# A two-layer message network and three graph attention layers on one core: messages by pairs of tiles, attention scores and row weights read from PSUM by VectorE

## The chip, the cores and the metric

The kernel runs on one core of one Trainium2 chip. The metric is the device time of one execution in microseconds (us). PE is TensorE, DVE is VectorE, ACT is ScalarE, POOL is GpSimd, and SP is the engine that issues most of the plain DMAs. A quad is four tiles of 128 edges, a pair is two tiles.

## The reference

The graph has 3125 nodes of 128 features and 100,000 edges. A residual network of two message layers comes first, and then a residual network of three GATv2 layers. The part of the reference that matters here:

```
def _block(h, src, dst, w, wm, bm, gm, bem, wu, bu, gu, beu, wg, bg):      # message layer, D = 160
    ecat = jnp.concatenate([h[src], h[dst]], axis=-1)
    em = jax.nn.relu(_layernorm(ecat @ wm.T + bm, gm, bem)) * w[:, None]
    msum = jax.ops.segment_sum(em, dst, num_segments=n)
    cnt = jax.ops.segment_sum(jnp.ones_like(w), dst, num_segments=n)[:, None]
    ...
def _gatv2_layer(x, src, dst, edge_e, Wl, bl, Wr, br, att_w, bias):        # 4 heads of 32
    gl = (x @ Wl + bl).reshape(n, HEADS, CH)
    gr = (x @ Wr + br).reshape(n, HEADS, CH)
    xj = gl[src]
    e = xj + gr[dst] + edge_e
    e = jax.nn.leaky_relu(e, negative_slope=0.2)
    alpha = jnp.einsum('ehc,hc->eh', e, att_w)
    m = jax.ops.segment_max(alpha, dst, num_segments=n)
    alpha = jnp.exp(alpha - m[dst])
    denom = jax.ops.segment_sum(alpha, dst, num_segments=n)
    alpha = alpha / (denom[dst] + 1e-16)
    out = jax.ops.segment_sum(xj * alpha[..., None], dst, num_segments=n)
    return out.reshape(n, HEADS * CH) + bias
```

## The kernel before

The program sorts the edges by destination once (0 to about 1600 us of the trace). After that each of the five edge layers walks the 812 tiles of 128 sorted edges in order, in 203 quads. The engines run programs written out by hand and meet only at semaphores, so that the order on each engine is the order of its source lines.

**Gathers.** For each tile POOL issues one indirect DMA that fetches 128 rows of a node table in HBM: L500 in the message layers (`ptab_d`, 160 columns), L508 in the attention layers (`gtab_d`, 132 columns). The gather of tile t waits until PE has summed quad t//4 - 8 (`s_sum` in the message layers, `s_e` in the attention layers), so that gathers run at most eight quads ahead.

**An attention layer** (`s_e` and the names below) runs in 217 rounds. In round j PE first does a step of a chunk's softmax if one is due. Then `scat` of quad j-14 (L1131) multiplies one-hot matrices by weighted rows into PSUM banks 6 and 7, after DVE has added what those banks held two pairs before (`s_acc2`). Then `pair(2j)` and `pair(2j+1)` follow: for each tile a matmul of a transposed one-hot with the node table block (L1144) and one that adds the gathered rows (L1147), 132 columns wide, into bank u % 3 for pair u. Each pair ends with a signal `s_e` and waits for the ACT copy of pair u-3 (`s_relu`). ACT copies the four linear columns (L876) and applies relu (L877) out of PSUM for each pair, converts the one-hots of quad j-12 (L892), and copies the row weights of quad j-13 from PSUM (L901). DVE multiplies gathered rows by weights (L1728, quad j-13), adds the four tiles of quad j-14 to the node sums (L1715), multiplies the relu by the attention vector (L1737) and reduces it to four scores for each edge (L1744). The softmax goes by chunks of eight quads: 26 chunks, whose steps (scans L1654 to L1657, carries L1667 to L1683, arguments L1690 to L1696, then the exponent and the weights' transpose) come in rounds 8c+9, +10, +11 and +12. Every second round begins on PE and on DVE with a load of eight register values (L426), the node block of each tile.

**A message layer** runs by quads: PE does `scat` of quad j-2 (L1061) and the sum of quad j (L1075 and L1078) into four banks. ACT takes the squares of each tile (L831) and one square root for the quad (L834), and scales the one-hots (L812). DVE does one reciprocal (L1539) and four normalising operations (L1545), then the adds (L1557).

**SP** loads the transposed one-hots and one-hots by eight tiles and, before the step of a chunk, that chunk's masks. The load of masks of chunk c waits until chunk c-2 is through.

Of the kernel before, what the change touches and what calls it, by code (L numbers as in the profile page):

```python
# [14 lines left out]
B = 112  # L15
# [8 lines left out]
NCH = (NQ + 7) // 8  # L24
TK = 32 * NCH
# [54 lines left out]
def gnn_program(nc, a, out):  # L80
    with ExitStack() as ctx:
# [12 lines left out]
        tabs_d = [nc.dram_tensor("ptab_d", (NP, D), F32).ap(), nc.dram_tensor("gtab_d", (NP, 132), F32).ap()]  # L94
# [7 lines left out]
        padc = sb("padc", [B, 1])  # L102
# [37 lines left out]
        BLb = carve(132, B)  # L140
        BRb = carve(132, B)
# [4 lines left out]
        attB = gB[:, 0:128]  # L146
        att2B = nbeB[:, 0:128]
        WLx = WPQ1[:, 0:132]
        WEx = WPQ1[0:16, D:D + 132]
# [5 lines left out]
        ring0 = cur[0]  # L155
        XJ = carve(32 * D)
        SQB = carve(6 * 512).rearrange("p (g k n) -> p g k n", g=6, k=4)
        NBB = carve(16 * B).bitcast(BF16).rearrange("p (g k n) -> p g k n", g=8, k=4)
        u0 = cur[0]
        RG = carve(4 * 8 * RW).rearrange("p (g t w) -> p g t w", g=4, w=RW)  # L160
        SW = carve(4 * 4 * B).rearrange("p (g k n) -> p g k n", g=4, k=4)
        VB = carve(3 * 644).rearrange("p (g k n) -> p g k n", g=3, k=4)
        JK = carve(D)
        SSQ = carve(4 * 8).rearrange("p (g n) -> p g n", g=4)
# [6 lines left out]
        RL = carve(2 * 512).rearrange("p (g n) -> p g n", g=2)  # L171
        AB = carve(2 * 528).rearrange("p (g k h c) -> p g k h c", g=2, k=4, h=4)
        PX = carve(3 * 528).rearrange("p (g k h c) -> p g k h c", g=3, k=4, h=4)
# [4 lines left out]
        PT = carve(2 * 128).rearrange("p (g n) -> p g n", g=2)  # L178
# [9 lines left out]
        SRC = carve(T).bitcast(I32)  # L188
        W = carve(T)
# [71 lines left out]
        HZ = AR[:, NB * 128:NB * 128 + 17 * 528]  # L261

        def xj2(t):

            s = (t // 4) % 24
            r = HZ[:, s * 528:(s + 1) * 528] if s < 17 else XJ[:, (s - 17) * 528:(s - 16) * 528]
            return r.rearrange("p (k f) -> p k f", k=4)
# [6 lines left out]
        TABG = tab_flat[:, 0:(NB + 1) * 132].rearrange("p (b f) -> p b f", f=132)  # L274
        Z132 = Z[:, :, 0:132]
# [5 lines left out]
        WRx = WU1[:, 0:132]  # L281
        gamB, betB, biB = guB[:, 0:128], beuB[:, 0:128], beB[:, 0:128]
        den = Zf[:, NB * 128:NB * 132].rearrange("p (b h) -> p b h", h=4)

# [12 lines left out]
        def bcF(v2):  # L297
# [26 lines left out]
        s_e, s_relu, s_att, s_lin = (sem(n) for n in ("s_e", "s_relu", "s_att", "s_lin"))  # L324
        s_at, s_s0, s_v, s_car, s_c, s_arg, s_pt, s_f, s_pb, s_r = (
            sem(n) for n in ("s_at", "s_s0", "s_v", "s_car", "s_c", "s_arg", "s_pt", "s_f", "s_pb", "s_r"))
        s_p, s_px, s_oh2, s_scat2, s_acc2, s_rs = (sem(n) for n in ("s_p", "s_px", "s_oh2", "s_scat2", "s_acc2", "s_rs"))
# [5 lines left out]
        def places(names):  # L333
# [13 lines left out]
        PL = places("ident0 ones ident iota dsti srci wraw padt0 padt1 padt lt0 lt rhs0 rhs iop pad0 pad tio onesN rmask0 rmask padc0 padc")  # L347
# [54 lines left out]
        def chunk_end(c):  # L402

            return min(8 * c + 8, NQ)
# [4 lines left out]
        def step_of(j, lag):  # L409

            c = (j - lag - 8) // 8
            return c if (j - lag) % 8 == 0 and 0 <= c < NCH else None

# [18 lines left out]
        def gpsimd_program(e):  # L432
# [3 lines left out]
            def mile(inst, name):  # L436
# [36 lines left out]
            mile(e.memset(padc[:, :], 0.0), "padc0")  # L473
            w.wait_own()
            mile(e.affine_select(out=padc[:, :], in_=padc[:, :], compare_op=ALU.is_gt, fill=BIG, base=LASTB,
                                 pattern=[[0, 1]], channel_multiplier=-1), "padc")
# [1372 lines left out]
```

## Time and profile before

| | before |
|---|---|
| runs | 8888.65, 8905.91, 8882.41 us |
| median | 8888.65 us |
| profiled execution | 8893.99 us |
| its span | 8891.9 us |
| busy in the span | PE 66%, weight loads 56%, DVE 51%, ACT 33%, POOL 53% |
| mean granted clock of TensorE | 0.831 |

The span runs from the first to the last instruction; the 2.1 us between it and the execution's own time lie around it. The profiled execution is 5.3 us above the median. Busy shares are means over a sort, two message layers, three attention layers and short stretches between them, so the profile is best read stage by stage.

### The profile page before, as it was taken

The page shows a single profiled execution, that of the slowest core. Times are in us where ns is not written, and L with a number is a line of the kernel's source. Part 1 is how long each engine was busy: PE and PEld are TensorE (multiplying, and loading weights), DVE is VectorE, ACT ScalarE, POOL GpSimd, SP SyncE. Part 2 cuts the span into 40 slices and gives each one's busy share as a digit, 9 for nine tenths or more (in the row PEclk, how much of TensorE's full clock was granted, in tenths as well). Part 3 has the DMA queues.
Part 4 walks back from the last instruction along what each step waited for, and adds up shares of the span by engine and source line. Part 5 has one row for each costly group of instructions (what it writes and reads, how often), then busy time and mean ns, then how long its engine had stood idle before and what let it go on. Part 6 is the DMA issues. An engine that isn't in the chain of part 4 may idle for free.

```text
span 8891.9 us, 116092 instructions
## 1 busy us (share of the span) xinstructions
PE 5832.2 (66%) x32977; PEld 4937.4 (56%) x32977; DVE 4515.0 (51%) x13873; ACT 2893.1 (33%) x12251; POOL 4707.3 (53%) x4869
## 2 busy tenths in 40 slices
PE   6544555677777867777775767763776673677775
PEld 5333333366767546666644666663666663666664
DVE  4222212255555446666643665664656664556666
ACT  2222221355555335555521222221222221222221
POOL 2665553366666046666505666634666652666660
PEclk9999999898888668888857888876888885788886
DMA  3000000333333134444403333332333341333331
GB/s 88 25 22 23 23 24 16 98 103 103 102 104 101 18 93 118 122 119 117 104 4 95 116 103 115 115 72 71 107 110 116 102 108 50 103 115 115 103 116 28
DMA packets 389512, 753.22 MB, mean 85 GB/s; under 512 B 101824, under 2 KB 248433, under 8 KB 388121
## 3 DMA queue, kind: packets, MB, share of 16 engines
q0 software_dynamic: 180928, 305.59, 14.7%
q1 hardware_dynamic: 203610, 425.90, 13.9%
q10 hardware_dynamic: 4352, 14.30, 0.6%
q8 instruction: 284, 4.65, 0.2%
q14 instruction: 338, 2.77, 0.1%
HBM read 639.02 MB, written 105.63 MB: 84 GB/s over the span
## 4 chain that ended last, share of the span: by engine, by line
PE 32%; another core or an unknown queue 23%; DVE 18%; issue 12%; ACT 12%; DVEq 2%; DMA 1%; ACTq 0%; SPq 0%; POOL 0%; POOLq 0%
PE PS L1131 5%; PE PS L1147 4%; ACT AR L831 4%; PE PS L1144 4%; PE PS L950 3%; DVE AR L1715 3%; PE PS L1061 2%; DVE AR L1737 2%; PE PS L1078 2%; PE PS L1075 2%; DVE AR L1557 2%; ACT AR L812 2%; DVE AR L1545 2%; DVE AR L1728 2%
## 5 line engine op out<-in xcount | busy, mean ns | idle before, releaser
L508 POOL DMA_INDIRECT AR<-gtab_d,AR x2436 | 2364.1, 970 | 1925.9 <-issue 642.2
L500 POOL DMA_INDIRECT AR<-ptab_d,AR x1624 | 1558.1, 959 | 1394.2 <-issue 415.1
L1131 PE MATMUL PS<-AR 128*112 128x132 f32 x4872 | 964.8, 342 | 604.9 <-DVE AR L1715 366.1
L1144 PE MATMUL PS<-AR 128*128 x4872 | 1182.3, 331 | 268.9 <-issue 141.6
L1131 PEld LDWEIGHTS PS<-AR 128*112 128x112 f32 x4872 | 766.7, 218 | 751.7 <-issue 512.5
L1147 PE MATMUL PS<-AR,ident 128*128 128x132 f32 x4872 | 1137.5, 321 | 23.2 <-DMA AR<-gtab_d,AR 13.5
L485 POOL DMA_INDIRECT rec_d<-AR x782 | 775.0, 991 | 662.3 <-DVE AR L1322 234.8
L1144 PEld LDWEIGHTS PS<-AR 128*128 128x128 f32 x4872 | 945.5, 239 | 315.0 <-issue 313.2
L1061 PE MATMUL PS<-AR 128*112 128x161 f32 x3248 | 697.7, 355 | 624.5 <-DVE AR L1557 334.6
L876 ACT ACTIVATE AR<-PS 128x8 f32<-128x8 f32 x1218 | 227.2, 187 | 2652.7 <-remote 1341.8
L1715 DVE TENSOR_TENSOR AR<-AR,PS 112x132 f32 x2436 | 710.2, 292 | 747.8 <-remote 247.4
L1147 PEld LDWEIGHTS PS<-AR,ident 128*128 128x128 f32 x4872 | 934.1, 236 | 28.8 <-DMA AR<-gtab_d,AR 16.3
L1061 PEld LDWEIGHTS PS<-AR 128*112 128x112 f32 x3248 | 534.2, 204 | 745.3 <-issue 357.5
L1075 PE MATMUL PS<-AR 112*128 x3248 | 825.9, 339 | 40.7 <-issue 22.3
L1737 DVE TENSOR_TENSOR AR<-AR 128x512 f32<-128x512 f32 x609 | 420.5, 690 | 814.7 <-ACT AR L877 503.9
L1078 PE MATMUL PS<-AR,ident 128*128 128x160 f32 x3248 | 797.2, 330 | 19.5 <-issue 19.4
L831 ACT ACTIVATE AR<-PS 128x160 f32<-128x160 f32 x1624 | 494.4, 304 | 961.8 <-remote 581.1
L1557 DVE TENSOR_TENSOR AR<-AR,PS 112x161 f32 x1624 | 522.8, 322 | 525.4 <-remote 261.0
L950 PE MATMUL PS<-AR 128*56 128x168 bf16 (+3 forms) x1369 | 379.3, 432 | 447.0 <-DVE AR L1338 322.3
L1075 PEld LDWEIGHTS PS<-AR 112*128 112x128 f32 x3248 | 631.7, 223 | 61.8 <-issue 61.7
L1078 PEld LDWEIGHTS PS<-AR,ident 128*128 128x128 f32 x3248 | 619.5, 219 | 22.3 <-issue 22.1
L950 PEld LDWEIGHTS PS<-AR 128*56 128x56 bf16 x1369 | 219.3, 191 | 564.1 <-DVE AR L1338 328.3
(323 smaller groups left out, 8832.2 us busy)
## 6 DMA issues: line engine op xcount, KB each, us to landing
AR<-ste_d SPq DMA_DIRECT2D x404, 512.0 KB
AR<-nbb_d SPq DMA_DIRECT2D x303, 224.0 KB
ste_d<-AR SPq DMA_DIRECT2D x101, 512.0 KB
AR<-gtab_d,AR POOLq DMA_INDIRECT x2436
AR<-ptab_d,AR POOLq DMA_INDIRECT x1624
nbb_d<-AR SPq DMA_DIRECT2D x101, 224.0 KB
AR<-key_d SPq DMA_DIRECT2D x94, 224.0 KB
rec_d<-AR POOLq DMA_INDIRECT x782
```

Source lines behind the costliest of these rows:

```text
L485: e.indirect_dma_start(out=rec_d[:, :], out_offset=bass.IndirectOffsetOnAxis(ap=rowi[:, n:n + 1], axis=0), in_=REC[:, c * RW:(c + 1) * RW] ...
L500: e.indirect_dma_start(out=XJ1[:, t % 32, :], out_offset=None, in_=tabs_d[0][:, :], in_offset=off).then_inc(done_, 16)
L508: e.indirect_dma_start(out=xj2(t)[:, t % 4, :], out_offset=None, in_=tabs_d[1][:, :], in_offset=off).then_inc(done_, 16)
L831: done(e.activation(JK, PS[(t // 2) % 4][:, (t % 2) * D:(t % 2 + 1) * D], ACT.Square, accum_out=SSQ[:, j % 4, kk:kk + 1]))
L950: return e.matmul(PS[3][0:KD, r0 * KD:r1 * KD].rearrange("p (k n) -> p k n", n=KD), x[:, 0:KD], x[:, KD:112].unsqueeze(1).to_broadcast([12 ...
L1061: x = e.matmul(PS[4 + v_ % 2][0:B, (t % 2) * 161:(t % 2 + 1) * 161], SW[:, i % 4, t % 4, :], VB[:, i % 3, t % 4, :], start=True, stop=True ...
L1075: e.matmul(o, STE[0:B, ste_slot(l, t), (t % 8) * 128:(t % 8 + 1) * 128], TABQ[0:B, bass.ds(block_of(cp, "tensor", t), 1), :], start=True, ...
L1078: x = e.matmul(o, ident[:, :], XJ1[:, t % 32, :], start=False, stop=True, skip_group_check=True)
L1131: x = e.matmul(PS[6 + v_ % 2][0:B, (t % 2) * 132:(t % 2 + 1) * 132], SQB[:, i % 6, t % 4, 0:B], PX[:, i % 3, t % 4, :, :].rearrange("p h c ...
L1144: e.matmul(o, STE[:, ste_slot(l + 2, t), (t % 8) * 128:(t % 8 + 1) * 128], TABG[:, bass.ds(block_of(cp, "tensor", t), 1), :], start=True, ...
L1147: x = e.matmul(o, ident[:, :], xj2(t)[:, t % 4, :], start=False, stop=True, skip_group_check=True)
L1715: x = e.tensor_tensor(o, o, PS[6 + v_ % 2][0:B, (t % 2) * 132:(t % 2 + 1) * 132].rearrange("p (a h c) -> p a h c", a=1, h=4), ALU.add)
```

## The change

**Attention layers.** The tables grow from 132 to 140 columns (`GW`): 35 for each head, which are 32 values, a column that holds one, and the linear sum with both signs. With an attention vector whose last three entries are 0, 1 and -1, a score is the sum of max(x, 0) times that vector, so that one DVE instruction for each pair (L1761 of the changed kernel, 128x280, input in PSUM) takes the place of L876, L877 and L1737. The product with the row weights (L1751) reads the weights in PSUM and writes 33 columns for each head, and L901 goes. PE's pairs wait for that DVE instruction, four banks deep (`s_att` of pair u-4), instead of for ACT's relu, three deep. The reduce (L1769) now reads 560 columns, and stands ahead of the adds. PX has five slots instead of three, and 29 quads of gathered rows are kept instead of 24. There are 27 chunks; the steps of a chunk lie two rounds apart, one round apart in the last four chunks, and the last chunks have four, four and three quads. Quad i is weighted in round i+17 (two in a round from round 193 on), where it was i+13; the layer has 214 rounds instead of 217. Mask loads stand elsewhere in SP's order.

**Message layers.** `scat`, the sums, the squares, the square root, the reciprocal and the adds go by pairs: `scat` of pair u-4 and the sum of pair u on PE, a square root and a reciprocal for each pair, adds of pair u-3. Making the masks is spread over the layer by sevens instead of eights.

```diff
-                for j in range(NQ + 14):
-                    for lag, step in ((1, scans), (2, carries), (3, args)):
+                for j in range(LASTR):
+                    for n, step in ((0, scans), (1, carries), (2, args)):
...
-                        w.wait_ge(s_p, quad_at(l, i))
+                        t0 = 4 * (i - chunk_start(chunk_of(i)))
+                        w.wait_ge(s_r, chunk_at(l, chunk_of(i)))
+                        if i >= 5:
+                            w.wait_ge(s_scat2, pair_at(l, 2 * (i - 5) + 1))
                         done(e.tensor_tensor(
-                            PX[:, i % 3, :, :, 0:32], xj2(4 * i)[:, :, 0:128].rearrange("p k (h c) -> p k h c", h=4),
-                            PX[:, i % 3, :, :, 32:33].to_broadcast([128, 4, 4, 32]), ALU.mult), s_px)
-                    if 14 <= j:
-                        add_quad(j - 14)
+                            PX[:, i % 5, :, :, :], xj2(4 * i).rearrange("p k (h c) -> p k h c", h=4)[:, :, :, 0:33],
+                            PS[4][:, 0:128].rearrange("p (h t) -> p t h", h=4)[:, t0:t0 + 4, :].unsqueeze(3).to_broadcast([128, 4, 4, 33]),
+                            ALU.mult), s_px)
                     if j < NQ:
-                        w.wait_ge(s_relu, pair_at(l, 2 * j + 1))
...
-                        done(e.tensor_tensor(
-                            AB[:, j % 2, :, :, 0:32], RL[:, j % 2, :].rearrange("p (k h c) -> p k h c", k=4, h=4),
-                            attB.unsqueeze(1).to_broadcast([128, 4, 128]).rearrange("p k (h c) -> p k h c", h=4), ALU.mult), s_att)
...
+                        for u in (2 * j, 2 * j + 1):
+                            w.wait_ge(s_e, pair_at(l, u))
...
+                            done(e.scalar_tensor_tensor(
+                                AB[:, j % 2, kk:kk + 2, :], PS[u % 4][:, 0:2 * GW].rearrange("p (k f) -> p k f", k=2), 0.0,
+                                attB.unsqueeze(1).to_broadcast([128, 2, GW]), ALU.max, ALU.mult), s_att)
...
+                    for i in weighted_in(j - 1):
+                        add_quad(i)
```

```diff
                     def pair(u):
-                        if u >= 3:
-                            w.wait_ge(s_relu, pair_at(l, u - 3))
+                        if u >= 4:
+                            w.wait_ge(s_att, pair_at(l, u - 4))
...
+def rounds_of_attention():
+    ends = list(range(8, 193, 8)) + [196, 200, NQ]
+    px, steps, start = [], [], 0
+    for c, end in enumerate(ends):
+        gap = 2 if c < 23 else 1
+        turn = end + gap
+        if steps:
+            turn = max(turn, steps[-1][2] + 1)
+        back = max(turn + 2 * gap + 1 + gap, px[-1] + 1 if px else 0)
+        steps.append((turn, turn + gap, turn + 2 * gap, turn + 2 * gap + gap - 1, back))
...
                         if t >= 32:
-                            w.wait_ge(s_sum, quad_at(layer, t // 4 - 8))
+                            w.wait_ge(s_sum, pair_at(layer, 2 * (t // 4 - 8) + 1))
```

On DVE, the middle of the first attention layer, before: a round's scores, product and adds, then the register load of the next round and its first add.

```order
L1737 TENSOR_TENSOR AR<-AR 128x16x32
L1744 TENSOR_REDUCE AR<-AR 128x4x4
L1728 TENSOR_TENSOR AR<-AR 128x16x32
L1715 ISA
L1715 TENSOR_TENSOR AR<-AR,PS6 112x132
```

The same place in the changed kernel (L1751 is the product, L1761 the score instruction of a pair, L1769 the reduce, L1735 an add):

```order
L1751 TENSOR_TENSOR AR<-AR,PS4 128x528
L1761 SCALAR_TENSOR_TENSOR AR<-PS0,AR 128x280
L1761 SCALAR_TENSOR_TENSOR AR<-PS1,AR 128x280
L1769 TENSOR_REDUCE AR<-AR 128x4x4
L466 TENSOR_LOAD AR
L1735 ISA
L1735 TENSOR_TENSOR AR<-AR,PS6 112x132
```

The scores read PSUM directly, a pair at a time, and the adds moved behind them.

On PE in the same stretch, before: `scat` of both pairs, the register load, and the first tile of the next quad.

```order
L1131 MATMUL PS6<-AR 112x132 x2
L1131 MATMUL PS7<-AR 112x132 x2
L426 TENSOR_LOAD AR
L1144 ISA
L1144 MATMUL PS0<-AR 128x132
L1147 MATMUL PS0<-AR,ident 128x132
```

In the changed kernel:

```order
L1145 MATMUL PS6<-AR 112x132 x2
L1145 MATMUL PS7<-AR 112x132 x2
L466 TENSOR_LOAD AR
L1158 ISA
L1158 MATMUL PS0<-AR 128x140
L1161 MATMUL PS0<-AR,ident 128x140
```

The order is the same; the pairs are 140 columns wide and go round four banks.

## Rows read from the trace of the kernel before

**Rows 1.** Busy time by stretch: a message layer, the second, an attention layer, its end.

```profile
core 0: us, PE busy (x) PEld busy (x) DVE busy (x) ACT busy (x) POOL busy (x), PEclk, DMA share, GB/s
1667.00:2940.00 1273.00, 945.81 (x5632) 865.75 (x5632) 683.95 (x2617) 735.84 (x3025) 769.01 (x801) 0.88 0.34 100
3197.00:4436.00 1239.00, 892.87 (x4882) 823.43 (x4882) 744.80 (x2979) 703.92 (x2850) 758.92 (x794) 0.85 0.41 116
4703.00:5993.00 1290.00, 879.82 (x5222) 790.82 (x5221) 742.82 (x1890) 293.14 (x1270) 784.39 (x805) 0.80 0.35 103
...
5911.00:5993.00 82.00, 58.91 (x318) 50.20 (x317) 57.30 (x163) 20.66 (x76) 0.00 (x0) 0.73 0.19 44
```

**Rows 2.** POOL's groups, 4800 to 5900 us (attention) and 1700 to 2900 us (messages).

```profile
L508 POOL DMA_INDIRECT AR<-gtab_d,AR x730 | 712.7, 976 | 386.1 <-issue 192.3 <-remote 108.5 <-PE PS L1147 82.9
...
L500 POOL DMA_INDIRECT AR<-ptab_d,AR x773 | 742.7, 961 | 460.4 <-issue 191.9 <-remote 175.8 <-PE PS L1078 92.7
```

**Rows 3.** POOL's timeline: start, duration, idle before it; three runs begin, one ends.

```profile
5012.81 0.94 POOL L508 DMA_INDIRECT AR<-gtab_d,AR  x1 [1.76 <-remote]
...
5021.68 0.95 POOL L508 DMA_INDIRECT AR<-gtab_d,AR  x1 [0.30 <-issue]
5024.65 0.95 POOL L508 DMA_INDIRECT AR<-gtab_d,AR  x1 [2.02 <-remote]
...
5036.49 0.95 POOL L508 DMA_INDIRECT AR<-gtab_d,AR  x1 [1.55 <-remote]
```

**Rows 4.** PE's timeline, the last pair of a quad.

```profile
5032.53 0.39 PE L1147 MATMUL PS<-AR,ident 128*128 128x132 f32 x2
```

**Rows 5.** ACT's timeline, the first instruction after that quad's pairs, both pairs.

```profile
5036.17 0.18 ACT L876 ACTIVATE AR<-PS 128x8 f32<-128x8 f32 x1 [8.04 <-remote]
...
5036.50 0.19 ACT L876 ACTIVATE AR<-PS 128x8 f32<-128x8 f32 x1
```

**Rows 6.** ACT's timeline at the start of the first attention layer.

```profile
4719.26 0.18 ACT L876 ACTIVATE AR<-PS 128x8 f32<-128x8 f32 x1 [11.53 <-remote]
...
4739.59 0.19 ACT L876 ACTIVATE AR<-PS 128x8 f32<-128x8 f32 x1 [19.88 <-remote]
...
4750.80 0.18 ACT L876 ACTIVATE AR<-PS 128x8 f32<-128x8 f32 x1 [10.75 <-remote]
```

**Rows 7.** POOL's timeline: the end and the beginning of its first pause there.

```profile
4743.32 0.95 POOL L508 DMA_INDIRECT AR<-gtab_d,AR  x1 [0.31 <-issue]
4751.03 0.94 POOL L508 DMA_INDIRECT AR<-gtab_d,AR  x1 [6.77 <-remote]
```

**Rows 8.** Waits, 4800 to 5900 us: us in total, times, longest.

```profile
ACT AR L876 <- remote: 378.5, 64, 8.5
ACT AR L876 <- PE PS L1147: 328.5, 142, 8.4
```

**Rows 9.** DVE's groups, 4800 to 5900 us.

```profile
L1715 DVE TENSOR_TENSOR AR<-AR,PS 112x132 f32 x720 | 209.9, 292 | 228.5 <-remote 90.9 <-issue 66.3 <-DVE AR L1715 41.7
L1744 DVE TENSOR_REDUCE AR<-AR 128x16 f32<-128x528 f32 x182 | 128.4, 705 | 6.2
L1737 DVE TENSOR_TENSOR AR<-AR 128x512 f32<-128x512 f32 x182 | 125.7, 690 | 175.4 <-ACT AR L877 90.8 <-issue 83.2
L1728 DVE TENSOR_TENSOR AR<-AR 128x512 f32<-128x512 f32 x181 | 123.6, 683 | 22.4 <-issue 22.4
...
L1657 DVE TENSOR_TENSOR AR<-AR 128x128 f32<-128x128 f32 x23 | 6.8, 294 | 0.8
L1696 DVE TENSOR_TENSOR AR<-PS,AR 128x128 f32<-128x128 f32 x23 | 6.7, 293 | 0.8
```

**Rows 10.** Groups of the message layer, 1700 to 2900 us: DVE's reciprocal, ACT's square root.

```profile
L1539 DVE RECIPROCAL AR<-AR 128x4 f32<-128x4 f32 x193 | 33.9, 176 | 247.3 <-ACT AR L834 230.1 <-issue 17.2
...
L834 ACT ACTIVATE AR<-AR,eps 128x4 f32<-128x4 f32 x193 | 57.7, 299 | 6.3
```

**Rows 11.** What SP's queue waited for, 4800 to 5900 us.

```profile
SPq L64 <- PE PS L1179: 375.0, 10, 39.3
```

More of the change, by code:

```diff
@@ L23 @@
 NG = (NQ + 1) // 2
-NCH = (NQ + 7) // 8
-TK = 32 * NCH
+HW = 35
+GW = 4 * HW
+TK = T + 32
+NXJ = 29
+def rounds_of_attention():
[8 more added lines that the diff above has]
+        steps.append((turn, turn + gap, turn + 2 * gap, turn + 2 * gap + gap - 1, back))
+        for i in range(start, end):
+            r = max(back + 1 - (c < 23), px[-1] if px else 0)
+            while px.count(r) >= (1 if r < NQ - 10 else 2):
+                r += 1
+            px.append(r)
+        start = end
+    return ends, steps, px
+ENDS, STEPS, PXR = rounds_of_attention()
+NCH = len(ENDS)
+LASTR = PXR[-1] + 3
 ROWS = 128 * T
@@ L139, in gnn_program @@
         WPQ2 = carve(2 * D, 33)
-        BLb = carve(132, B)
-        BRb = carve(132, B)
+        BLb = carve(GW, B)
+        BRb = carve(GW, B)
         BPQ = BLb[0:1, :]
@@ L400, in half, with chunk_start, chunk_of, step_of @@
             return min(8, T - 8 * g8)
-        def chunk_end(c):
-            return min(8 * c + 8, NQ)
+        def chunk_start(c):
+            return ENDS[c - 1] if c else 0
+        def chunk_of(i):
+            return next(c for c in range(NCH) if i < ENDS[c])
         def chunk_at(layer, c):
             return layer * NCH + c + 1 if c >= 0 else 0
-        def step_of(j, lag):
-            c = (j - lag - 8) // 8
-            return c if (j - lag) % 8 == 0 and 0 <= c < NCH else None
+        def step_of(j, n):
+            return next((c for c in range(NCH) if STEPS[c][n] == j), None)
+        def weighted_in(j):
+            return [i for i in range(NQ) if PXR[i] == j]
         def load_of(c):
@@ L603, in sync_program @@
                     e.dma_start(LD[:, 0:T], DL[127:128, :]).then_inc(s_lk, 16)
-                    for g8 in range(NG + 8):
+                    for g8 in range(NG + 10):
                         if g8 < NG:
@@ L649, in sync_program @@
                         read_ste(e, w, l + 2, g8)
-                    if g8 == 0 or g8 % 4 == 2 and g8 // 4 + 1 < NCH:
-                        load_masks(e, w, l, 0 if g8 == 0 else g8 // 4 + 1)
-                    o8 = g8 - 5
+                    if g8 < 2:
+                        load_masks(e, w, l, g8)
+                    for c in range(2, NCH):
+                        if g8 == (4 * c + 4 if c < 24 else 100 + 2 * (c - 24)):
+                            load_masks(e, w, l, c)
+                    o8 = g8 - 7
                     if o8 >= 0:
@@ L1499, in tile_rows @@
                     w.wait_own()
-                    for x, r in ((AM, 0), (E2, 31), (EM, 31)):
-                        v(e.memset(x.rearrange("p (c t) -> p c t", t=32)[:, :, r:r + 1], BIG))
+                    for end in ENDS:
+                        v(e.memset(AM[:, 4 * end:4 * end + 1], BIG))
+                        for x in (E2, EM):
+                            v(e.memset(x[:, 4 * end - 1:4 * end], BIG))
+                    v(e.memset(AM[:, 0:1], BIG))
+                    for x in (E2, EM):
+                        v(e.memset(x[:, TK - 1:TK], BIG))
                     w.wait_own()
@@ L1558, in vector_program @@
                                 acc_done = w.done(x, s_acc if t % 2 else None)
+                        if 0 <= u < 2 * NQ:
+                            w.wait_ge(s_rms, pair_at(l, u))
+                            v(e.reciprocal(SSQ[:, u % 8, 0:2], SSQ[:, u % 8, 2:4]))
+                            if u >= 6:
+                                w.wait_ge(s_scat, pair_at(l, u - 6))
+                            w.wait_own()
+                            for t in (2 * u, 2 * u + 1):
+                                x = e.scalar_tensor_tensor(
+                                    VB[:, u % 6, t % 2, 0:D], PS[u % 4][:, (t % 2) * D:(t % 2 + 1) * D],
+                                    SSQ[:, u % 8, t % 2:t % 2 + 1], nbeB, ALU.mult, ALU.max)
+                            done(x, s_vt)
                 w.wait_ge(s_tab, 16 * (l + 1))
```

351 lines of the change are left out of this document (159 added, 192 removed), and 6 rows, old and new, of the table DV.

## The prediction

> **What bounds the kernel now.** I read the busy times by stretch first, to see whether any engine is full. None is: in an attention layer of 1290 us PE is busy for 880, DVE for 743, POOL for 784 and ACT for 293, and in a message layer of 1273 us no engine reaches 950 [rows 1]. So the pace is set by engines waiting for one another, and the next view is POOL's, since POOL does the same work in all five edge layers. 730 gathers in 1100 us are 12.05 us for eight (two quads, 6.03 us each); the 773 of the message layer in 1200 us are 12.42 us for eight, 6.21 each [rows 2]. The two kinds of layer have quite different work on PE, ACT and DVE, and yet nearly the same pace. Of each period the gathers themselves take 8 x 1.25 = 10.0 us, and then POOL stands still for about 2 us until PE has signalled the quad that frees the next slots: runs begin at 5012.81, 5024.65 and 5036.49 us, twice exactly 11.84 us apart [rows 3].
>
> Why is PE's signal late? PE's last pair of a quad stands in the trace at 5032.53 us and ends at 5032.92 [rows 4]. ACT, which has nothing else to do, starts on the first pair of that quad at 5036.17 and on the second at 5036.50, after 8.04 us of idleness [rows 5]. At least 0.9 us of matmuls lie between the two pairs on PE; their signals reach ACT 0.33 us apart or closer. So it is not the matmuls that are late but what others see of them, and it comes out in a bunch just before POOL starts again. The start of a layer shows the same without the pauses: POOL issues gathers without a stop until 4744.3 us [rows 7], and ACT gets to a pair after 11.5, 19.9 and 10.8 us of waiting, at 4719.26, 4739.59 and 4750.80 [rows 6]; then all is ready at once and POOL goes on at 4751.03. In the largest waits of the layer ACT waits 378.5 us for a releaser that the trace doesn't name, and 328.5 us for L1147 [rows 8]; that is 707 of 1100 us.
>
> My reading, which the trace suggests but doesn't prove: while POOL issues gathers back to back, PE's progress is seen late, and POOL must pause for PE to catch up. Eight gathers and one pause make 12 us, whatever DVE and ACT do in between. The change leaves the gathers, the eight-quad window and PE's order as they are.
>
> **The change part by part, attention layers.** Two rows price DVE's new shapes: 512 columns take 0.690 us (L1737), 128 columns 0.294 us (L1657), so 1.03 ns a column [rows 9]. A score instruction of 280 columns is then 0.294 + 152 x 0.00103 = 0.451 us; it reads PSUM, which costs nothing more, since L1696 (PSUM) takes 0.293 us where L1657 (SBUF) takes 0.294 for the same 128 columns [rows 9]. The reduce grows by 32 columns (+0.033) and the product by 16 (+0.017). For each quad DVE loses L1737 (0.690) and gains 0.902 + 0.050: +0.262 us, 53 us for 203 quads. DVE's occupancy now is 743/203 = 3.66 us of work and, in the stretch of rows 9, 108 us of short gaps at L1715 over 182 quads, 0.59: 4.25 of 6.03 us. It becomes 4.5, still below the 5.0 of four gathers. I count these 53 us at nothing, because the idle 1.8 us a quad covers them; if the cover is gone they cost 53 us a layer.
>
> The Trainium skill, "VectorE: DVE Perf Modes", section on the TRN2 errata, gives a PSUM source 62 cycles more of fixed cost on VectorE than an SBUF source. By that page the two score instructions and nothing else would be some 0.13 us a quad dearer, 26 us a layer; L1696 against L1657 contradicts it here.
>
> ACT loses L876, L877 and L901. It was waiting 707 us anyway [rows 8], so the direct worth is nothing; what could be worth something is the hop, PE to ACT to DVE, which becomes PE to DVE. That shortens what follows the late signal by one relu pair and adds nothing to when the signal comes. PE gets four banks instead of three for pairs. Its pairs are 140 instead of 132 columns: two thirds of its matmuls get 6% longer, 880 x 2/3 x 0.06 = 35 us a layer of busy time, beside 410 us idle. The mask loads leave SP blocked for 375 us of 1100 [rows 11]; no engine's largest wait is for what SP loads, so moving them is worth nothing. Chunk steps two rounds apart spread DVE's work: 743 - 203 x (4 x 0.292 + 0.705 + 0.690 + 0.683) = 84 us, 3.2 us for each of 26 chunks. They are off the path while gathers run.
>
> **The end of a layer** has no gathers, and there DVE counts. The window from the landing of the last gather to the last add is 82 us; DVE is busy for 57.3 [rows 1], and with 22 quads of adds at 0.59 us of gaps it is occupied for 70. At that point before has 22 quads to weight and add (the lag is 14 rounds); the change has 25 (17 rounds and one). That is 3 x (0.70 + 4 x 0.292 + 0.59) = 7.4 us, one more chunk's steps 3.2, and 8 rounds of scores at 0.26, 2.1: +12.7 us of DVE's work, of which the 12 idle us may hide some. I take 11 a layer, bounds 0 and 15 (with 6% of PE's 59 us), 33 in all. Packing two quads to a round from round 193 shortens the count of rounds by three, not the work.
>
> **Between the layers** the weights' preparation has some 14 more small DVE instructions in series. The nearest row is the reciprocal of 4 columns, 0.176 us [rows 10]: 2.5 us a layer, 7.5 in all; bounds 0 and, with the weight loads in 32-column pieces, 6 a layer.
>
> **Message layers.** A second reciprocal (0.176) on DVE and a second square root (0.299) on ACT for each quad [rows 10] are 36 and 61 us a layer, beside 589 and 537 us idle [rows 1]: nothing. Working by pairs ends the layer perhaps half a quad earlier, 3 us; bounds 0 and 6. The gathers wait for the same quad as before.
>
> **Sum.** 8894.0 + 33 + 7.5 - 6 = 8928.5 against the profiled execution; that one lies 5.3 us above the median of the runs, so 8923.
>
> **Rivals.** *The chain was the bound (faster).* If the period is in truth the round trip PE, ACT, DVE, PE, the change cuts a hop out of it, adds a bank, and by pairs does the same for the messages. For it: ACT waits for L1147 in 328.5 us, and no engine is full. Against it: the equal period of unlike layers, 11.84 us twice to the hundredth, and the bunched signals. Rounds of 5.5 us, halfway between 6.0 and the gathers' 5.0, give 3 x 195 x 0.53 = 310 us and in the messages 195 x (0.71 + 0.6) = 255 (the second message layer at 6.1 by its 1239 us): 8923 - 565 = 8358. With the gathers as the only bound it would be 7870; with a pause a tenth of a microsecond or two shorter, some 8800.
>
> *The late signals starve DVE (slower).* DVE now meets PE directly: it can't score before `s_e` is seen, PE's banks stay taken until it has, and it stands in order before the adds that free `scat`'s banks. If of each 12 us DVE can work only the 8 or so between a late bunch and the next, its 9.0 us for two quads no longer fit in the round that also carries a chunk's step, and its added 53 us come out in full: 3 x 53 = 159, 9082; with PE's 35 a layer as well, 9187. It decides when the slack of 1.5 us a quad is less than what DVE must wait for PE.
>
> *The change does less than it says.* DVE's reduce, product and adds stay in one queue, so that dropping ACT's work moves no wait. That is the forecast.
>
> **How the numbers follow.** Pace kept, 0.45: 8880 to 8960, of which two fifths lie within 0.3% of before (26.7 us, about what a measurement of this kernel can tell from no change) and nearly all the rest above. Chain, 0.35: 7870 to 8860. Starved DVE, 0.20: 8960 to 9190. Together: faster 0.36, same 0.20, slower 0.44. The likeliest is 8923. The range has to leave out no more than 2 in 10: below 8400 I see 0.13 and above 9120 0.05, so 8400 to 9120.
>
> **What would show it.** If the pace is kept, eight gathers take 11.8 to 12.1 us in the changed kernel's attention layers, POOL's pause stays near 2 us, DVE rather than ACT shows the long waits for PE (over 250 us in 1100), and the end of a layer grows from 82 to about 93 us. The chain rival shows in runs of more than eight gathers, or pauses under 1 us. The starved DVE shows in pauses of 3 us with DVE busy before them. I am wrong if the 280-column instruction takes over 0.6 us, or if PE's banks, not its signals, were what POOL waited for.

## The result, and the profile after

The changed kernel takes 9004.36 us (median of four runs, 8999.17 to 9005.93) beside 8895.42 us for the kernel before (8882.41 to 8905.91): ratio 1.0122, 95% interval 1.0105 to 1.014. It is slower by 1.2%. The forecast was 8923 us, slower, in a range of 8400 to 9120. The direction is right and the time lies in the range, but the loss is three times the one that was summed up: 105 us between the profiled executions, where the sum had 34.5.

| us, profiled executions | before | after | difference |
|---|---|---|---|
| gathers, first to last, message layer 1 | 1251.1 | 1300.2 | +49.1 |
| the same, message layer 2 | 1227.6 | 1236.4 | +8.8 |
| the same, three attention layers | 3645.9 | 3588.7 | -57.2 |
| last gather to last add, three attention layers | 240.6 | 336.0 | +95.4 |
| last add to the next layer's first gather, twice, or to the end | 307.8 | 314.7 | +6.9 |
| last gather to last add, two message layers | 78.6 | 72.3 | -6.3 |
| everything else (the sort, +4.6; the stretch ahead of the first attention layer, +4.2) | | | +8.6 |
| span | 8891.9 | 8997.2 | +105.3 |

Three rows carry it, and they have different signs: the first message layer's gathers and the ends of the attention layers are longer, and the attention layers' gathers are shorter. The busy times of the changed kernel by stretch, in the columns of [rows 1]: the two message layers, the first attention layer, and that layer's end.

```profile
1672.00:2992.00 1320.00, 914.33 (x5638) 875.01 (x5638) 718.28 (x2823) 796.73 (x3230) 759.30 (x801) 0.85 0.34 96
3238.00:4494.00 1256.00, 862.16 (x4897) 796.11 (x4896) 779.01 (x3290) 764.80 (x3057) 759.82 (x801) 0.86 0.40 115
4755.00:6064.00 1309.00, 897.80 (x5250) 794.86 (x5250) 779.04 (x2111) 122.15 (x258) 765.95 (x812) 0.82 0.36 105
5953.00:6064.00 111.00, 70.38 (x383) 60.38 (x381) 71.66 (x213) 14.73 (x32) 0.00 (x0) 0.75 0.12 23
```

No engine is full here either. ACT has fallen from 293 to 122 us in the attention layer, and the layer is 19 us longer.

POOL's group in the changed kernel, 4860 to 5940 us, answers to [rows 2]:

```profile
L544 POOL DMA_INDIRECT AR<-gtab_d,AR x730 | 688.7, 943 | 392.0 <-issue 195.4 <-remote 126.1 <-PE PS L1161 70.6
```

It is 730 gathers in 1080 us, 11.84 us for eight; the pauses for PE (126.1 + 70.6 us) are as long as before (108.5 + 82.9; over all three layers POOL's idle time beyond the usual 0.3 us between gathers is 551 us where it was 543), but the mean gather is 943 ns, where it was 976. POOL's timeline, against [rows 3]:

```profile
5001.66 0.94 POOL L544 DMA_INDIRECT AR<-gtab_d,AR  x1 [0.30 <-issue]
5004.83 0.94 POOL L544 DMA_INDIRECT AR<-gtab_d,AR  x1 [2.23 <-remote]
...
5013.56 0.94 POOL L544 DMA_INDIRECT AR<-gtab_d,AR  x1 [0.30 <-issue]
5016.68 0.94 POOL L544 DMA_INDIRECT AR<-gtab_d,AR  x1 [2.17 <-remote]
```

Eight gathers, a pause of 2.2 us, a period of 11.85 us: the pace is kept. Who waits has changed. In the waits of 4860 to 5940 us DVE now meets PE's late signal itself, 226 us in all, where ACT waited 707 us [rows 8]:

```profile
DVE AR L1761 <- PE PS L1161: 124.8, 46, 5.9
...
DVE AR L1761 <- remote: 101.3, 47, 5.9
```

DVE's new shapes, by its groups in the same stretch, against [rows 9]:

```profile
L1761 DVE SCALAR_TENSOR_TENSOR AR<-PS,AR 128x280 f32<-128x280 f32 x362 | 145.4, 442 | 226.3 <-PE PS L1161 124.8 <-remote 101.3 <-issue 0.3
L1769 DVE TENSOR_REDUCE AR<-AR 128x16 f32<-128x560 f32 x181 | 133.7, 739 | 6.2
L1751 DVE TENSOR_TENSOR AR<-AR,PS 128x528 f32<-128x528 f32 x176 | 122.4, 696 | 0.1
```

They came out at 0.442, 0.739 and 0.696 us, and were priced at 0.451, 0.738 and 0.700.

### The profile page after: what moved, and what is told of

It is laid out like the page before. It is cut to its first block, busy times and chain, and to the rows that moved or that the text cites. A ratio compares the mean times of both kernels' runs of the same rounds, so it can differ in the third digit from the quotient of the medians.

```text
span 8997.2 us, 115195 instructions
## 1 busy us (share of the span) xinstructions
PE 5829.8 (65%) x33021; PEld 4939.4 (55%) x33021; DVE 4690.3 (52%) x15073; ACT 2500.8 (28%) x9619; POOL 4620.2 (51%) x4867
## 4 chain that ended last, share of the span: by engine, by line
PE 18%; DVE 17%; issue 14%; another core or an unknown queue 10%; ACT 3%; DVEq 2%; DMA 1%; SPq 0%; ACTq 0%
PE PS L1145 4%; DVE AR L1735 4%; PE PS L1161 4%; PE PS L1158 3%; DVE AR L1761 2%; DVE AR L1751 2%; PE PS L1075 1%; DVE AR L1562 1%; DVEq L466 1%; PE PS L1092 1%; DVEq L1735 1%; PE PS L1089 1%; ACT AR L872 1%; DVE AR L1494 1%
## 5 line engine op out<-in xcount | busy, mean ns | idle before, releaser
L544 POOL DMA_INDIRECT AR<-gtab_d,AR x2436 | 2298.4, 944 | 2005.2 <-DMA gtab_d<-AR 712.1
L1158 PE MATMUL PS<-AR 128*128 x4872 | 1202.6, 334 | 255.1 <-issue 174.1
L1161 PE MATMUL PS<-AR,ident 128*128 128x140 f32 x4872 | 1167.9, 324 | 86.9 <-issue 68.6
L1735 DVE TENSOR_TENSOR AR<-AR,PS 112x132 f32 x2436 | 709.9, 291 | 603.1 <-DVE AR L1735 247.1
L1761 DVE SCALAR_TENSOR_TENSOR AR<-PS,AR 128x280 f32<-128x280 f32 x1218 | 491.4, 442 | 968.6 <-remote 499.4
L919 ACT ACTIVATE AR<-AR 128x448 f32<-128x448 bf16 x609 | 336.4, 571 | 1944.7 <-remote 1171.9
L1089 PE MATMUL PS<-AR 112*128 x3248 | 803.8, 332 | 32.5 <-issue 32.0
L1089 PEld LDWEIGHTS PS<-AR 112*128 112x128 f32 x3248 | 613.4, 217 | 47.5 <-issue 45.4
L1571 DVE SCALAR_TENSOR_TENSOR AR<-PS,AR 128x160 f32<-128x160 f32 x1624 | 549.2, 380 | 33.6 <-remote 3.2
```

Source lines behind the costliest of these rows:

```text
L544: e.indirect_dma_start(out=xj2(t)[:, t % 4, :], out_offset=None, in_=tabs_d[1][:, :], in_offset=off).then_inc(done_, 16)
L1089: e.matmul(o, STE[0:B, ste_slot(l, t), (t % 8) * 128:(t % 8 + 1) * 128], TABQ[0:B, bass.ds(block_of(cp, "tensor", t), 1), :], start=True, ...
L1158: e.matmul(o, STE[:, ste_slot(l + 2, t), (t % 8) * 128:(t % 8 + 1) * 128], TABG[:, bass.ds(block_of(cp, "tensor", t), 1), :], start=True, ...
L1161: x = e.matmul(o, ident[:, :], xj2(t)[:, t % 4, :], start=False, stop=True, skip_group_check=True)
L1735: x = e.tensor_tensor(o, o, PS[6 + v_ % 2][0:B, (t % 2) * 132:(t % 2 + 1) * 132].rearrange("p (a h c) -> p a h c", a=1, h=4), ALU.add)
L1761: done(e.scalar_tensor_tensor(AB[:, j % 2, kk:kk + 2, :], PS[u % 4][:, 0:2 * GW].rearrange("p (k f) -> p k f", k=2), 0.0, attB.unsqueeze(1 ...
```

## The experiments

The runs fell on at least three chips, which are of two kinds, and this has to be known first. On that of the measurement above and of the first four experiments (called chip A, a single chip or ones that run alike) the kernel before takes 8882 to 8936 us. On the two other chips (B for the next four, C for the last four) it takes 7387 to 7418 us. Only ratios to the kernel before on the same chip are compared across them.

**Plain loads instead of gathers** (chip A). ACT issues the loads of the attention layers; what they fetch is not what the edges need.

```diff
+                        r = 37 * t % 2880
+                        e.dma_start(xj2(t)[:, t % 4, :], tabs_d[1][r:r + 128, :]).then_inc(s_pl[(l * NQ + i) % 8], 16)
...
-                        e.indirect_dma_start(out=xj2(t)[:, t % 4, :], out_offset=None, in_=tabs_d[1][:, :],
-                                             in_offset=off).then_inc(done_, 16)
```

> The changed kernel, in whose attention layers ACT issues plain DMAs of 128 neighbouring rows of the table (same bytes, slots and window of eight quads) in place of POOL's indirect gathers; the rows are not those of the edges. The message layers keep POOL's gathers. Theory A (POOL's issuing of gathers is what makes PE's signals late): without it the 203 quads of an attention layer go at 4.5 to 5.0 us each instead of 5.93, so that the stretch from the first to the last load falls from 1196 to 900 to 1000 us a layer, and DVE's long waits for PE go. Theory B (the round trip between PE and DVE sets the pace, whoever loads): 1170 to 1210 us a layer, unchanged.

Measured: 8088.43 us, 916 less than the changed kernel. DVE's reduces, one for each quad, come every 4.66 to 4.69 us between quads 20 and 190 instead of every 5.93. In DVE's groups of 4900 to 5500 us (129 quads) the wait of the score instruction for PE has shrunk to 5.5 us:

```profile
L1775 DVE SCALAR_TENSOR_TENSOR AR<-PS,AR 128x280 f32<-128x280 f32 x258 | 103.8, 439 | 5.6 <-PE PS L1175 5.5
L1783 DVE TENSOR_REDUCE AR<-AR 128x16 f32<-128x560 f32 x129 | 95.3, 738 | 4.4
```

The signals themselves can be timed in the trace, from the end of a pair's last matmul to the start of the instruction that waits for it. Here 99 of the 100 waits of the score instruction end 0.04 us behind the matmul; in the changed kernel 243 of 331 end more than 3.5 us behind. So on this chip PE's signals are late with POOL's gathers and in time without them, the bytes, slots and window being the same. DVE is then the bound: of the 600 us it is busy or in the short gaps before its adds for all but some 16, at 4.66 us a quad, which the prediction had at 4.5. The run changes three things at once, though: the engine that issues, the kind of DMA (indirect or plain), and the rows (scattered or neighbouring). Which of them makes the signals late isn't separated; theory A names the first.

**A window of ten quads** (chip A).

```diff
-                        if t >= 32:
-                            w.wait_ge(s_e, pair_at(layer - 2, 2 * (t // 4 - 8) + 1))
+                        if t >= 40:
+                            w.wait_ge(s_e, pair_at(layer - 2, 2 * (t // 4 - 10) + 1))
```

> The changed kernel with gathers of the attention layers allowed ten quads ahead of PE instead of eight (40 semaphores instead of 32). Theory A: after a longer first run (48 gathers without a pause instead of 40) the same 11.8 to 11.9 us for eight gathers, since POOL still has to stop for PE; 1190 to 1200 us a layer. Theory B, or a latency from a gather's issue to its use that the window must cover: 1/5 shorter, down to the 10.0 us of the gathers alone; 1010 to 1100 us a layer.

Measured: 9051.61 us. POOL's group, 4870 to 5950 us:

```profile
L544 POOL DMA_INDIRECT AR<-gtab_d,AR x727 | 687.7, 946 | 392.9 <-issue 194.5 <-remote 136.7 <-PE PS L1161 61.7
```

The pace is the same (11.88 us for eight; 1198 to 1200 us a layer), and from the last gather to the last add it is 122 us instead of 112. A latency that the window has to cover is ruled out: it forecast 1010 to 1100 us a layer. More slots only leave more quads to finish when the gathers are over.

**A fixed node block on PE** (chip A), so that PE loads no register values in the attention layers; the scores are those of wrong nodes.

```diff
-                                     TABG[:, bass.ds(block_of(cp, "tensor", t), 1), :], start=True, stop=False, skip_group_check=True)
+                                     TABG[:, 0:1, :], start=True, stop=False, skip_group_check=True)
```

> The changed kernel, in whose attention layers PE takes block 0 of the node table for every tile, so that its loads of eight register values (every second quad) and its register operations go; scores are those of other nodes. Theory C (PE's loads of register values are what gets stuck while POOL issues, since the late pairs are those behind such a load): the late signals go and eight gathers take 10.0 to 10.8 us, 1010 to 1090 us a layer. Theory A in general: unchanged, 1185 to 1197 us.

Measured: 9009.15 us, 1195 to 1197 us a layer, and in POOL's group (4860 to 5940 us) the same pauses. PE's register loads are not what makes the signals late.

```profile
L544 POOL DMA_INDIRECT AR<-gtab_d,AR x730 | 690.7, 946 | 390.2 <-issue 193.9 <-remote 131.7 <-PE PS L1161 63.4
```

**Message layers by quads again** (chip A, timed). The parts of PE, ACT and DVE in the message layers, and the gather's wait, are put back as before:

```diff
-                            w.wait_ge(s_sum, pair_at(layer, 2 * (t // 4 - 8) + 1))
+                            w.wait_ge(s_sum, quad_at(layer, t // 4 - 8))
...
-                        done(e.activation(SSQ[:, u % 8, 2:4], SSQ[:, u % 8, 0:2], ACT.Sqrt, bias=eps[:, :], scale=1.0 / D), s_rms)
+                        done(e.activation(SSQ[:, j % 4, 4:8], SSQ[:, j % 4, 0:4], ACT.Sqrt, bias=eps[:, :], scale=1.0 / D), s_rms)
```

> The changed kernel with the message layers' sums, squares, roots, reciprocals and adds by quads, as before; the attention layers as changed. If working by pairs is what made the first message layer longer (gathers 1251 us before, 1300 us after; the second 1228 and 1236), they go back to 1245 to 1255 and 1225 to 1231 us and the kernel takes 8940 to 8955 us, ratio to before 1.005 to 1.007. If the masks by sevens or the memory's new layout did it: no change, ratio 1.011 to 1.013.

Measured: 8968.47 us, ratio 1.0067 (1.0045 to 1.009); the layers' gathers take 1250.8 and 1232.9 us. The ratio and the first layer are as expected; the second layer (1225 to 1231 us expected) and the time (8940 to 8955) came out a little longer. Nearly half of the loss belongs to the pairs, and nearly all of that to the first message layer. POOL's group in that layer, 1700 to 2900 us, of the changed kernel and of this run:

```profile
L536 POOL DMA_INDIRECT AR<-ptab_d,AR x741 | 703.3, 949 | 497.2 <-PE PS L1092 198.8 <-issue 181.7 <-remote 116.7
```

```profile
L536 POOL DMA_INDIRECT AR<-ptab_d,AR x774 | 736.7, 952 | 464.2 <-issue 192.3 <-remote 182.7 <-PE PS L1089 89.2
```

The pauses are 315 us for 741 gathers by pairs and 272 for 774 by quads.

**A window of six quads** (chip B, timed).

```diff
-                        if t >= 32:
-                            w.wait_ge(s_e, pair_at(layer - 2, 2 * (t // 4 - 8) + 1))
+                        if t >= 24:
+                            w.wait_ge(s_e, pair_at(layer - 2, 2 * (t // 4 - 6) + 1))
```

> The changed kernel with gathers of the attention layers allowed six quads ahead of PE instead of eight. Theory A (POOL pauses because PE's signals come late while it issues, not for lack of slots): the period of eight gathers stays 11.8 to 11.95 us, and a layer ends sooner, because only six quads instead of eight are left to score after the last gather: 2 x 4.9 = 10 us a layer, as ten quads cost 12 more. From the last gather to the last add 100 us instead of 112; kernel 8965 to 8980 us, ratio to before 1.006 to 1.008. Theory B (the window must cover a latency): the period grows by up to a third, 12.5 us or more, and the kernel takes over 9050 us.

Measured: 7371.58 us, ratio 0.9961 (0.9947 to 0.9975). POOL doesn't pause at all on this chip: eight gathers in 9.99 us, 1014 us a layer. The window is never reached, so this run can't answer its question, and nothing of the 10 us a layer that were expected of it can come: the changed kernel on chip C has 80.5 us from last gather to last add and this one 81.

**Chunk steps one round apart** (chip B, timed).

```diff
-        gap = 2 if c < 23 else 1
+        gap = 1
```

> The changed kernel with the steps of a chunk one round apart in all chunks, so that quad i is weighted in round i+13 as before; 27 chunks with the small last ones stay. If the lag of 17 rounds is what makes a layer's end longer (four quads more to weight and add, 4 x 2.45 us): the stretch from the last gather to the last add falls from 112 to 100 to 103 us, and gathers keep 11.8 to 11.95 us for eight; kernel 8970 to 8985 us, ratio 1.006 to 1.009. If the two rounds were needed to keep DVE clear of PE: eight gathers take 12.1 us or more and the kernel 9020 us.

Measured: 7341.19 us, ratio 0.9918 (0.9902 to 0.9935). From the last gather to the last add it is 69.3 us, 11 less than the changed kernel's 80.5 on chip C (and the 81 of the run before on this chip), and the gathers keep 1014 us. The lag of four more rounds costs 11 us a layer and buys nothing where this could be seen. On chip A it wasn't run.

**One more DVE instruction, with one input in SBUF, and with two** (chip B).

```diff
+                        if 1 <= j < 190:
+                            x = AB[:, j % 2, :, :]
+                            v(e.tensor_reduce(JUNK[:, 0:16], x.rearrange("p k (h c) -> p (k h) c", h=4), AX.X, ALU.add))
```

> The changed kernel with one more DVE instruction in each round of an attention layer up to round 189, a reduce of 560 columns with one input in SBUF, 0.74 us, whose result is not used (and a wait for DVE's own work). Theory A: DVE's 4.7 us of work a quad become 5.4, still under the 5.93 of the gathers' pace: gathers 11.85 to 12.2 us for eight. If DVE is the bound beside POOL: 0.7 us more a quad, 13.3 us for eight. Gathers keep their mean of 0.944 us.

```diff
+                            v(e.tensor_tensor(JUNK.bitcast(BF16), x.rearrange("p k f -> p (k f)")[:, 0:512], x.rearrange("p k f -> p (k f)")[:, 48:560], ALU.add))
```

> The same with a DVE addition of 512 columns whose two inputs are in SBUF, 0.69 us, like L1737 of the kernel before. If such an instruction holds up POOL's gathers (before: 98 gathers of over 1.1 us in the attention layers, the changed kernel none): 80 to 150 gathers of over 1.1 us come back in the attention layers and their mean rises from 0.944 to 0.965 to 0.985 us. If they came from something else: none, as in the run with one input.

Measured: 7509.91 and 7491.08 us. With one input the reduces of quads 20 to 190 come every 5.26 to 5.28 us instead of 4.99 to 5.00, and POOL pauses 17 to 19 times a layer, 14 to 15 us in all. The added instruction's 0.73 us a quad came out as 0.27, so on this chip DVE had less than 0.5 us a quad to spare before it is the bound. (The 11.85 and 13.3 us for eight gathers that were expected belong to chip A.) With two inputs the gathers themselves grow. The attention gathers of the whole trace, one input and then two:

```profile
L545 POOL DMA_INDIRECT AR<-gtab_d,AR x2436 | 2304.0, 946 | 1480.1 <-issue 695.3 <-DMA gtab_d<-AR 694.3 <-PE PS L1162 77.5
```

```profile
L545 POOL DMA_INDIRECT AR<-gtab_d,AR x2436 | 2336.5, 959 | 1430.3 <-issue 702.9 <-DMA gtab_d<-AR 688.2 <-PE PS L1162 26.1
```

6 gathers of over 1.1 us with one input, 95 with two. The mean rose by 13 ns, less than the 21 expected at least, the count fell within what was expected. So DVE instructions with two SBUF inputs hold up gathers. The timeline shows which ones: all 88 gathers that began 0.1 to 0.4 us after the start of the added two-input instruction took over 1.1 us, and none of the 95 that began so behind the added one-input instruction. The Trainium skill, "SBUF — State Buffer", section "SBUF: two separate sides", has the rule: VectorE and GpSimd share a pair of ports by an exclusive lock, which a VectorE instruction with two SBUF inputs takes against a GpSimd instruction that reads SBUF. By that rule, the trace agrees as far as the gathers go: in the trace of before 94 of the 98 long attention gathers ran beside L1737, whose two inputs lie in SBUF, and the other 4 beside L1728, which has two as well; the changed kernel's L1761 and L1751 take one input from PSUM, and none of its 2436 attention gathers there is over 1.1 us. DVE's side shows no hold-up: the 609 L1737 of before took 0.68 to 0.73 us each, those that began while a gather was under way too.

**The changed kernel, and the kernel before** (chip C, the first timed).

> The changed kernel itself, beside the kernel before on one chip, because chips differ: on one, before takes 8890 to 8910 us and POOL pauses 2 us after every eight gathers; on another it takes 7396 us and POOL does not pause. Where POOL pauses: ratio 1.010 to 1.014. Where it does not, the attention layers' gathers take 1014 us in both kernels, DVE's chain can't be the bound in either, and only the ends of the layers differ (some 15 to 30 us each) and the message layers' do not: ratio 1.005 to 1.013. If dropping ACT from the chain had a worth that the pauses hid, the ratio there is under 1.000.

> The kernel before itself, for its trace on the same chip as the others. Where POOL does not pause: eight gathers in 10.0 to 10.1 us in all five layers, save for gathers held up beside two-input instructions of DVE (mean 0.97 us instead of 0.945, 20 us a layer); from the last gather to the last add 60 to 75 us. Where it pauses: 11.9 us and 80 to 82 us.

Measured: 7363.26 us for the changed kernel beside 7395.6, ratio 0.9951 (0.9933 to 0.9969): on this chip it is the faster one, where 1.005 to 1.013 was expected. The trace of before (7393.15 us) shows ACT's and POOL's waits of 3900 to 4800 us so:

```profile
ACT AR L876 <- PE PS L1147: 562.8, 316, 5.3
POOL AR L508 <- issue: 202.7, 665, 0.3
PEld PS L1147 <- DMA AR<-gtab_d,AR: 154.0, 166, 2.9
```

POOL waits for nobody, and PE waits for gathers. In this trace each of the 1107 relu instructions that followed idleness came 0.04 us behind PE's last matmul; on chip A, of 793 such a quarter came more than 3.5 us behind, and the latest 39 us. The late signals aren't there on chips B and C, although POOL issues its gathers there with even fewer pauses; in the changed kernel too every wait for a pair ends 0.04 us behind it. The gathers of the two kernels, 3900 to 4800 and 3900 to 4750 us:

```profile
L508 POOL DMA_INDIRECT AR<-gtab_d,AR x702 | 685.9, 977 | 214.0 <-issue 202.7 <-PE PS L1147 9.1 <-DVE AR L1728 2.1
```

```profile
L544 POOL DMA_INDIRECT AR<-gtab_d,AR x681 | 643.4, 945 | 207.6 <-issue 195.7 <-PE PS L1161 10.1 <-DVE AR L1751 1.8
```

On this chip 181 of before's attention gathers are over 1.1 us, 3 of the changed kernel's. 32 ns a gather are 26 us a layer: 1040.6 us from first to last gather before, 1013.6 after, -81 for three. The message layers' gathers go from 1031.7 to 1017.6 us, -28 for two. The layers' ends take that back in part: 55.8 us before, 80.5 after, +74 for three. With 5.5 us between the layers the sum is -29.5; -32.3 was measured. My expectation there had left out the gathers held up by DVE, though I had written them into the next one; that one had them at 0.97 us and 20 us a layer, and had 60 to 75 us for the layers' ends, which are 55.8. Its other outcome, a ratio under 1.000 because ACT is out of the chain, gets no support: POOL waits for nobody in either kernel here, and the shorter gathers make up the gain.

**The message layers by quads and the steps one round apart, with 27 chunks and then with 26** (chip C, timed).

```diff
+                    if 1 <= j <= NQ:
+                        i = j - 1
+                        w.wait_ge(s_rms, quad_at(l, i))
...
-        gap = 2 if c < 23 else 1
+        gap = 1
```

> The changed kernel with the message layers by quads as before and the chunk steps one round apart; 27 chunks. Both undone parts cost something in the runs so far (0.55% for the pairs where POOL pauses; the steps' lag at the ends of the layers). Sum of the two where POOL pauses: 8967 - 3 x 10 = 8937 us, ratio 1.002 to 1.006, 112 us from the last gather to the last add down to 100. Where it does not pause: ratio 0.988 to 0.995, since before's gathers are held up there by DVE and the new kernel's are not.

```diff
-    ends = list(range(8, 193, 8)) + [196, 200, NQ]
+    ends = list(range(8, 201, 8)) + [NQ]
```

> The same with 26 chunks, the last of 8, 8 and 3 quads as before, instead of 27 with 4, 4 and 3 at the end. If the four chunk steps packed into the last rounds are what makes the end long (3.2 us of DVE and a round of waits for PE for each): another 5 to 15 us off each layer's end, and the kernel 15 to 40 us faster than the run with 27 chunks; 1.000 to 1.003 of before where POOL pauses. If the small last chunks are worth having, because weights come earlier: 5 to 10 us a layer slower than it.

Measured: 7366.01 us (ratio 0.9955, 0.9941 to 0.9969) and 7354.70 us (0.9932, 0.9909 to 0.9956). Both end the layers sooner, 69.2 and 65.0 us against 80.5. Both expectations were a little too good: the first ratio was to be 0.988 to 0.995, and 26 chunks were to take another 5 to 15 us off each end and 15 to 40 off the time, where 4 and 11 were measured. The last gather and the last adds of the first attention layer with 26 chunks:

```profile
4821.36 0.94 POOL L544 DMA_INDIRECT AR<-gtab_d,AR  x1 [0.30 <-issue]
```

```profile
4887.12 0.29 DVE L1734 TENSOR_TENSOR AR<-AR,PS 112x132 f32 x1 [0.15 <-DVE AR L1734]
```

The small last chunks cost 4 us a layer instead of gaining any. But both runs lose the message layers' 28 us, which the pairs had gained on these chips: by quads their gathers are held up again (84 of over 1.1 us in the first of the two runs, 4 in the changed kernel). 80 of those 84 stand beside L1491, which compares destinations for the one-hots; by pairs the same instruction runs as often and makes no gather that long. Why wasn't separated. The lowest ratio to before is that of the run with pairs and the steps one round apart, 0.9918 (0.9902 to 0.9935), but its interval overlaps that of the run with 26 chunks, and they ran on two chips. The version that suggests itself, pairs with the steps one round apart and 26 chunks, wasn't run.

## Why the prediction was right, and where it was not

**The total owes something to luck.** The sum had three terms wrong by 57 to 62 us each, one of them in the other direction; without that one the kernel would have come out near 9060 us.

**The pace was kept: right, and the reason holds for chip A.** I forecast 11.8 to 12.1 us for eight gathers and a pause near 2 us, and 11.84 and 2.2 were measured; the waits moved from ACT to DVE, though with 226 us they fell short of the 250 that I had named. Three experiments on the same chip tie it to POOL's gathers: without them the lateness is gone, and a larger window or no register loads change nothing. Whether it is POOL's issuing, as I wrote, or the indirect DMAs themselves, and why PE's signals are late there, stays open; that it is not so on every chip was outside everything I had considered.

**DVE's 53 us cost nothing while gathers ran: right** on chip A, where POOL's pauses stayed at 551 us against 543. The new instructions' prices were right within 2%. The product L1751 reads PSUM too, which the prediction left out when it said that only the two score instructions would be dearer by a fixed cost of PSUM; with 0.696 us against 0.700 without such a cost it is no dearer either.

**The attention gathers as a fixed 8 x 1.25 us: wrong.** They became 19 us a layer shorter. [Rows 2] held the sign: its mean was 976 ns, where a single gather in [rows 3] takes 0.94 or 0.95; in the three layers 98 gathers of over 1.1 us, 50 us longer than the others in all, make nearly all of that difference, and DVE's two-input L1737 stood beside them. The two runs with an added instruction show it. Over three layers this term was 57 us that the sum lacks.

**The end of a layer: right in kind, sized 11 us, measured 31.8.** The work was counted well: DVE's busy time rose from 57.3 [rows 1] to 71.7 us, 14.4, where I had 12.7 with the gaps. The step that failed was to let DVE's idle time there hide some of it. It grew instead, from 24.7 to 39.3 us. DVE's waits for PE's `scat` in the layer's end, before (5911 to 5993 us) and in the changed kernel (5953 to 6064 us), and the three longest of the latter in its timeline:

```profile
DVE AR L1715 <- PE PS L1131: 7.3, 11, 1.0
```

```profile
DVE AR L1735 <- PE PS L1145: 20.5, 23, 3.3
```

```profile
6024.75 0.29 DVE L1735 TENSOR_TENSOR AR<-AR,PS 112x132 f32 x1 [3.33 <-PE PS L1145]
...
6034.11 0.29 DVE L1735 TENSOR_TENSOR AR<-AR,PS 112x132 f32 x1 [3.00 <-PE PS L1145]
...
6045.26 0.29 DVE L1735 TENSOR_TENSOR AR<-AR,PS 112x132 f32 x1 [3.32 <-PE PS L1145]
```

Each stands behind a step of one of the last, small chunks. In the first and the third DVE has just weighted two or four quads, and PE's `scat` of the first of them starts only when the products are done; in the second PE does its own step of the chunk first, which waits for DVE's carries. DVE has nothing to do in between. Also at the last gather 26 to 27 quads were still to be added (106 adds of a tile), not the 25 I counted. (The schedule comes to 213 rounds, four fewer than before's 217 and not three; the work is the same.) Chip C, where no signal is late, lets the ends grow by 25 us, so most of this isn't the lateness.

**Between the layers: 2.5 us forecast ahead of each attention layer, 4.2, 4.0 and 3.2 measured.**

**Message layers: wrong.** I had them 6 us shorter by pairs. Their ends are indeed 6.3 us shorter on chip A, but their gathers, which I took to be unchanged, take 58 us longer, and undoing the pairs takes most of it back (1300 to 1251 us in the first). The step that failed was to price two more small instructions and call the rest the same because "the gathers wait for the same quad as before". In the first message layer POOL's pauses are a response to PE, ACT and DVE, not a fixed sum: its pace was 12.42 us for eight [rows 2] and not 11.9, and it became 1200/741 x 8 = 12.96. Which of the pairs' waits lengthens it wasn't separated. On chip C, where POOL doesn't pause, the pairs cost nothing and the gathers are 14 us a layer shorter.

**Starved DVE** (rival, 0.20) didn't come about; **the chain** (0.35) neither: without gathers the new chain does run at 4.66 us a quad, but while POOL gathers, nothing of that reaches the time. Between the profiled executions the loss is 71 us above the sum: 58 for the messages' gathers, 95 - 33 for the ends, less 57 for the attention gathers, 4.6 for a sort that took that much longer in this execution, and 3 to 4 for the preparation of the weights. The other 10 us of the 81 between 9004 and 8923 come from taking medians: the profiled execution of before lay 5.3 us above its median, and that of the changed kernel 5.2 below.

## What to carry to other kernels

Where unlike stages run at one pace, look for what they share, and time that alone before shortening what they don't: on chip A dropping 58% of an engine's work in a layer moved nothing, and putting plain loads in the place of POOL's gathers moved 900 us. Read a group's mean against the single instruction in the timeline: 976 against 945 ns was worth 57 us, more than the chain that the change rewrote. And when work is put off by some rounds, price the end of the loop, where each postponed quad and each small last step stands bare. Last, run a kernel on more than one chip before explaining a wait: the order of these two turned with it.

## What the runs showed of the hardware

Chips differ far more than any change here: the same kernel takes 8882 to 8936 us on chip A and 7387 to 7418 us on two others. The difference is in the sort, with POOL's scatters (450 us of it for before on chip C), and in the five layers with their gathers; the stretches between the layers, which have neither, agree within 1.5 us. On chip A the instructions that wait for PE in the attention layers start up to 39 us behind its matmul while POOL issues indirect DMAs back to back, and 0.04 us behind it when ACT issues plain ones. What differs in the chips isn't known. The order of two kernels can turn with it, 1.0122 on the one and 0.9951 on the other. A DVE instruction of 0.68 us with two SBUF inputs in each round made 95 of 2436 gathers longer than 1.1 us, all those among them that began 0.1 to 0.4 us behind its start; a reduce with one SBUF input, and L1751 and L1761 with one of their inputs in PSUM, held none up.
